# The last two groups of a fused decoder layer as expert chunks of their own, and the order of work after the last attention step

## What is computed

```python
x = _layernorm(x + attn(x))            # causal conv, minGRU scan, gelu feed-forward
x = _layernorm(x + xattn(x, ctx))      # cross attention, 16 heads of 64, causal mask
router = sigmoid(x @ gate_w + gate_b)  # 16 experts
values, indices = top_k(router, k=2)
values = values / sum(values)
x = _layernorm(x + shared_mlp(x) + sum_k values[k] * expert_mlp[indices[k]](x))
```

## Time and profile before

| | us |
|---|---|
| median of 3 runs | 1592.21 (1584.35 to 1595.37) |
| the profiled execution | 1589.19 |
| its span in the trace | 1587.5 |
| transposes of group 15 for the router begin (PE L417) | 1461.98 |
| slots of the last chunk written (DVE L1367) | 1476.67 |
| last scatter issued (POOL L1623) | 1496.18 |
| last `d_down` (PE L711) begins | 1537.13 |
| last gather issued (POOL L1635) | 1576.27 |

### The profile page before, as it was taken

The page is one execution under the profiler, slowest core; times in us unless marked ns, Lnnn a source line. Parts: engine busy times, 40 slices in busy tenths (PEclk is TensorE's granted clock), DMA queues, the critical chain, the costliest instruction groups (busy, mean ns, idle before and its releaser), DMA issues. The chain is left out here.

```text
span 1587.5 us, 34224 instructions
## 1 busy us (share of the span) xinstructions
PE 1327.4 (84%) x11168; PEld 1077.3 (68%) x11168; DVE 1021.0 (64%) x2723; ACT 876.1 (55%) x3255; POOL 834.0 (53%) x996
## 2 busy tenths in 40 slices
PE   2879797989899998989888998989889898986550
PEld 1667676777777776777777776867767777765540
DVE  3566657566756777667766767666776767666233
ACT  3656555565665665565655656565655655553120
POOL 4353334553446546664566545664566545564345
PEclk9999899999999999999999999999999999999685
DMA  6000000032112212132122212133122222133651
GB/s 211 8 7 8 7 8 14 10 92 81 36 57 69 84 57 60 47 105 85 36 63 83 81 54 65 44 94 95 36 65 76 81 64 64 33 95 104 183 156 46
DMA packets 142897, 105.78 MB, mean 67 GB/s; under 512 B 12352, under 2 KB 137856, under 8 KB 142720
## 3 DMA queue, kind: packets, MB, share of 16 engines
q1 hardware_dynamic: 132224, 84.71, 18.3%
q0 software_dynamic: 8192, 16.79, 3.6%
q10 hardware_dynamic: 2304, 2.10, 0.4%
HBM read 69.99 MB, written 33.55 MB: 65 GB/s over the span
## 5 line engine op out<-in xcount | busy, mean ns | idle before, releaser
L1595 POOL TENSOR_TENSOR pr<-pr,ri 128x480 f32<-128x480 f32 x256 | 250.4, 992 | 267.3 <-DVE ri L1229 265.3
L919 ACT ACTIVATE pr<-sE,nm 128x120 f32<-128x120 f32 x512 | 177.6, 359 | 292.1 <-DVE nm L1215 292.1
L591 PE MATMUL pvb<-pT,vv 120*64 120x128 f32 x2048 | 143.2, 283 | 42.9 <-DVE pT L1225 42.6
L919 ACT ACTIVATE pr<-sO,nm 128x120 f32<-128x120 f32 x512 | 178.8, 381 | 0.0
L558 PEld LDWEIGHTS sE<-kT,qT 64*128 64x128 f32 x1024 | 127.7, 193 | 54.8 <-issue 54.8
L591 PEld LDWEIGHTS pvb<-pT,vv 120*64 120x64 f32 x2048 | 112.5, 139 | 72.5 <-DVE pT L1225 55.3
L1635 POOL DMA_INDIRECT gat<-sorted_y,slot x128 | 127.1, 993 | 64.3 <-issue 47.1
L1623 POOL DMA_INDIRECT sorted_x<-x,slot x128 | 128.1, 1001 | 49.4 <-issue 34.6
L558 PE MATMUL sE<-kT,qT 64*128 64x120 f32 x1024 | 151.6, 290 | 0.0
L558 PE MATMUL sO<-kT,qT 64*128 64x120 f32 x1024 | 151.6, 290 | 0.0
L417 PE MATMUL t<-ident_f,pr 128*120 128x128 f32 x1024 | 146.6, 290 | 1.8 <-POOL pr L1595 1.4
(11 more groups left out here) (334 smaller groups left out, 3535.5 us busy)
## 6 DMA issues: line engine op xcount, KB each, us to landing
wq<-in_w_e SPq DMA_DIRECT2D x224, 128.0 KB
sorted_y<-yq SPq DMA_DIRECT2D x64, 256.0 KB, 2.5
xq<-sorted_x SPq DMA_DIRECT2D x56, 256.0 KB, 2.8
xt<-in_x SPq DMA_DIRECT2D x16, 256.0 KB, 3.0
sorted_x<-yq SPq DMA_DIRECT2D x16, 256.0 KB, 4.0
out_y<-y SPq DMA_DIRECT2D x64, 64.0 KB, 1.6
cT<-in_ctxT SPq DMA_DIRECT2D x16, 240.0 KB, 3.0
sorted_x<-x,slot POOLq DMA_INDIRECT x128
```

The source lines that it names most:

```text
L591: ins = mm(pvb[r * DK:(r + 1) * DK, (k // 2) * T:(k // 2 + 1) * T], vv[:, q, h * DK:(h + 1) * DK], pT[:, 4 * r + k // 2, :], start=True, s ...
L919: ins = f(pr[:, p % RING, r, i, :], score_banks[r][:, i * S:(i + 1) * S], ACT.Exp, bias=nm[:, p % 2, r, i:i + 1], accum_out=rsum[:, p % 2, ...
L1595: GP.tensor_tensor(pr[:, p % RING, r, :, :], pr[:, p % RING, r, :, :], ri[:, p % 2, r, :, :].to_broadcast([P, 4, S]), ALU.mult).then_inc(s ...
```

## The change

**Chunks.** Groups 0 to 13 keep their seven chunks of two groups. Groups 14 and 15 become a chunk each (`LONE`), of 24 tiles, six quads: quads 56 to 61 are group 14, quads 62 to 67 group 15. So the last two groups have 12 quads where they had 8. Slots, ranks and scatters of such a chunk are over four sequences (8 scatters).

**Step 15.** It now does all eight quads of chunk 6 (48 to 55), one per sub-step from 2 to 9 (`up_in`), with `d_down` into a bank of its own (`ma`), so that `d_up` no longer waits for `d_y` of the quad before. `c_slots` of group 14 is done at sub-step 1, and its eight scatters at sub-steps 3 to 6. On SP the loads of weights stand ahead of the stores of the sums. At its sub-steps 8 to 10 SP loads the rows of quads 56 to 59 and the weights of 56 to 58.

**After the attention.** There is no step 16. Every engine has a list written out: stage C of group 15 with quads 56 to 59 between its pieces, then the other quads and the sums of groups 12 to 15 (`TAIL` = 12). The sums there have buffers of their own (`gat_last`, `ys_last`, `y_last`), four sequences at a time, and `e_ln4` makes the reciprocal roots of four at once. The sorted outputs are in three memory buffers instead of two. ACT loads the weights of quads 65 to 67.

```diff
+LONE_TILES = 24
+DEEP = G // 2 - 2
+LONE = G // 2 - 1
+LAST = LONE * TILES // QUAD
+LONE_QUADS = LONE_TILES // QUAD
+END = LAST + 2 * LONE_QUADS
+TAIL = G - 4
...
+        def x_last_in(n):
+            i = n - LAST
+            return ("xq_last0", LONE_QUADS) if i < LONE_QUADS else (f"xq_last{1 + (i - LONE_QUADS) // 3}", 3)
+        def w_last_in(n):
+            i = n - LAST
+            return ("wq_last0", 3) if i < 3 else ("wq_last1", 3) if i < LONE_QUADS else (f"wq_last{2 + (i - LONE_QUADS) // 3}", 3)
...
+        def up_in(d, s):
+            if d is None:
+                return None
+            if d == G - 4:
+                return QUADS * d + s - 2 if 2 <= s < 2 + 2 * QUADS else None
+            return QUADS * d + s // 2 - 1 if s % 2 == 0 and 2 <= s <= 2 * QUADS else None
...
+                if d == G - 4:
+                    n = QUADS * d
+                    for s in range(2, PAIRS + LAG + 1):
+                        if n + s < LAST:
+                            x_load(n + s)
+                        if s > 2:
+                            if n + s - 1 < LAST:
+                                w_load(n + s - 1)
+                            d_store(n + s - 3)
+                        for e, q in sums_in(es, s - 1):
+                            e_store(e, q)
+                        if s == 8:
+                            for name in ("a_bank", "ln1_out"):
+                                sp.wait_ge(sem[name], whole(name, G - 1))
+                            for i in range(4):
+                                x_load(LAST + i)
+                        if s >= 8:
+                            w_load(LAST + s - 8)
...
             pipeline(body)
+            n = LAST + LONE_QUADS
             for i in range(2):
+                sp.wait_ge(sem["dT"], upto("dT", 0, LAST - 2 + i))
+                x_load(LAST + 4 + i)
+            w_load(LAST + 3)
...
             def d_T(n, c=None):
                 if last(n):
-                    pe.wait_ge(sem[f"xq_last{(n - LAST) // 4}"], 64)
+                    pe.wait_ge(sem[x_last_in(n)[0]], 16 * x_last_in(n)[1])
...
             def d_up(n, c=None):
                 if last(n):
-                    pe.wait_ge(sem[f"wq_last{(n - LAST) // 2}"], 32 * QUAD)
+                    pe.wait_ge(sem[w_last_in(n)[0]], 16 * QUAD * w_last_in(n)[1])
...
             pipeline(body)
-            for i in range(quads + 2):
+            c = G - 1
+            d_down(LAST - 1)
+            d_T(LAST)
+            d_T(LAST + 1)
+            c_x2_T(c)
+            d_up(LAST)
+            c_router_shared(c)
+            d_up(LAST + 1)
+            d_down(LAST)
+            c_shared_T(c)
+            d_T(LAST + 2)
+            d_up(LAST + 2)
+            d_T(LAST + 3)
+            c_rank(LONE + 1)
+            c_shared_down(c)
+            d_down(LAST + 1)
+            d_up(LAST + 3)
...
             pipeline(body)
-            for e in (G - 4, G - 2):
-                for j in range(0, 2 * SEQ + 2, 2):
...
+            gathers([TAIL], 0, 2 * SEQ)
+            for n in range(2 * SEQ):
+                c_scatter(LONE + 1, n)
+            e_ln4(TAIL)
+            gathers([TAIL + 1], 0, 2 * SEQ)
+            gathers([TAIL + 2], 0, SEQ)
+            e_ln4(TAIL + 1)
+            gathers([TAIL + 2], SEQ, 2 * SEQ)
+            gathers([TAIL + 3], 0, SEQ)
+            e_ln4(TAIL + 2)
+            gathers([TAIL + 3], SEQ, 2 * SEQ)
+            e_ln4(TAIL + 3)
```

More of the change, by code:

```diff
@@ L192, in layer_kernel @@
         wide = 2 * I + P
[L193 to L196, removed]
-        hq_last = gin[:, 0:2 * P].rearrange("p (v n) -> p v n", v=2)
+        half = QUAD * P
@@ L741, in body @@
                         b_scores(b, s)
-                    if D and s > 1 and odd:
-                        d_down(QUADS * d + (s - 3) // 2)
-                    if D and s > 1 and not odd:
-                        d_up(QUADS * d + s // 2 - 1, c)
+                    if up_in(d, s - 1) is not None:
+                        d_down(up_in(d, s - 1))
+                    if up_in(d, s) is not None:
+                        d_up(up_in(d, s), c if s == 2 else None)
                     if A and s == 8:
@@ L759, in body @@
                         c_shared_down(c)
-                    if C and s == 1 and c % 2:
-                        c_rank(c // 2)
-                    if D and odd and s < 9:
-                        d_T(QUADS * d + (s - 1) // 2, c)
+                    if C and s == 1 and closes(c):
+                        c_rank(chunk_of(c))
+                    if up_in(d, s + 1) is not None:
+                        d_T(up_in(d, s + 1), c if s == 1 else None)
                     if A and s == 8:
@@ L782, in _ @@
             pipeline(body)
-            for i in range(quads + 2):
-                if i < quads:
-                    d_T(LAST + i)
-                if 0 < i <= quads:
-                    d_up(LAST + i - 1)
-                if i > 1:
-                    d_down(LAST + i - 2)
+            c = G - 1
[15 more added lines that the diff above has]
+            d_up(LAST + 3)
+            for n in range(LAST + 4, END + 2):
+                if n == LAST + LONE_QUADS:
+                    d_down(n - 2)
+                    d_down(n - 1)
+                if n < END:
+                    d_T(n)
+                if n > LAST + LONE_QUADS:
+                    if n <= END:
+                        d_up(n - 1)
+                    if n > LAST + LONE_QUADS + 1:
+                        d_down(n - 2)
+                elif n < LAST + LONE_QUADS:
+                    d_down(n - 2)
+                    d_up(n)
         @block.scalar
@@ L1366, in c_slots @@
                         dve.wait_ge(sem[f"gath{q}"], whole(f"gath{q}", 2 * (k - 3) + 1))
[L1367 removed]
+                V.tensor_copy(slot[k % 3][:, :, some], sf[:, :, some]).then_inc(sem["slots"], 1)
             def d_act(n):
@@ L1456, in body @@
                         c_base(c)
-                    if C and s == 1 and c % 2:
-                        c_slots(c // 2)
-                    if D and s > 1 and not odd:
-                        d_act(QUADS * d + s // 2 - 1)
+                    if C and s == 1 and closes(c):
+                        c_slots(chunk_of(c))
+                    if up_in(d, s) is not None:
+                        d_act(up_in(d, s))
                     for e, q in sums_in(es, s - 1):
```

440 lines of the change are left out of this document (275 added, 165 removed).

## The result

The changed kernel takes 1584.47 us (median of 6 runs, 1581.79 to 1587.23), the kernel before on the same chip 1592.5 (1584.35 to 1595.37): a ratio of 0.9956, 95% interval 0.9935 to 0.9977. Run again beside some of the experiments, it stood at 0.9959 (0.9944 to 0.9975). So it is 0.4% faster, 5.6 us by the later medians and 8.0 by the first, which is "within 1%", the likeliest of the three; the forecast was 1580. The profiled execution has a span of 1581.6 us, where the sum said 1575.5 and before it was 1587.5.

The account below looks back on a forecast made before the run. The end was taken as bound by a chain of hand-overs, no engine full. Points timed in sequence gave a span of 1575.5 against 1587.5 (−12), 1577.2 profiled, 1580 on the median's scale; range 1564 to 1594.

Parts of the forecast that it names:

- (a): Step 15, sub-step 1: group 14's slots are new there, partly hidden by DVE idle time; +2.3 us, bounds 0.7 to 3.3.
- (b): Step 15: `d_act` at every sub-step instead of every second, 0.79 us at sub-steps 3, 5 and 7; +2.4 us.
- (c): Step 15: additional PE work, some 3 us per sub-step pair, hidden while PE waits for exponentials; uncovered up to 3 per pair.
- rival 3: Step 15: the loop of weights sets the pace, each of six sub-steps 2.8 us more; +17, 1597 us; chance 0.08.
- (d): Step 15, sub-steps 3 to 6: eight scatters on POOL, 2.5 us per sub-step, hidden by slack; 0, at most 1 us.
- `d_down(53)` and the list of SP: `d_down(53)` ends at 1453.7; SP then issues loads and stores to 1476.6, rows land 1480.0, PE stalls about 13 us.
- Rows to slots: From landed rows at 1480.0 to group 15's slots at 1501.1: 1.8 + 19.3 us, at a granted clock of 0.50.
- rival 2: Step 15 hardly grows and PE runs at full clock soon after the stall; −4 and −5, 1571 us; chance 0.17.
- Quads 57 to 59: After group 15's ranks: `d_y(57)` out at 1502.9, `d_y(59)` at 1517.1, with copies 7.1 us apart.
- Rows of 62 to 64: After the stores and weights in SP's list: third load of rows starts at 1523.0 and lands at 1526.4.
- Last six quads and last gathers: Kernel's end: last quads take 26.7 us, stored at 1553.1; last gather starts at 1563.3, span ends at 1575.5.
- Rival 1: After step 15: transfers, not SP's issuing, set the loads' pace; everything from 1480.0 up to 13 us earlier, 1567; chance 0.12.

## Why the prediction was right, and which of its steps were off

The median came out 4.5 us above the forecast, inside the range, and the likeliest class was the right one. By its steps, all on the old clock:

- **(a), slots in step 15:** predicted +2.3, measured +2.64.
- **(b), `d_act` at every sub-step:** predicted 0.79 each; 0.72 in the run with the scatters moved away.
- **(c), more PE work:** 0, as predicted. In step 15 PE waited 8.4 us for DVE's copies and never for a load (1395 to 1470); rival 3, weights as the pace, did not come.
- **(d), scatters at 0: the step that failed.** They cost 6.2 us by sub-step 7, 2.0 to 2.1 in each of the three intervals that hold a stretched instruction. "Whose next instructions have a sub-step of slack" was wrong: a cycle of POOL is roots, two gathers, two scatters, two multiplications and the root's wait for DVE's statistics (`mv`), and with the scatters it takes 8.9 and 11.0 us where the pace had been 7.5. The stretched `y` of the earlier trace rows was in my hands as a sign of that coupling, and I took it for a cost of `y` instead of a cost that grows when POOL is late.
- **`d_down(53)` and the list of SP.** It ended at 1459.6 (1457.68 + 1.94) instead of 1453.7. SP began the weights of 55 only 2.35 us behind it, where 0.7 had been taken, since a store of a sum stood ahead of them whose `y` was the 2.43 us one. From the end of their issue (1463.67) to the load of the rows of 61 (begun at 1486.2) the list took 22.6 us where 18.6 were summed: 1.2 more for the two stores, 1.5 more for the rows of 56 to 59, and 1.1 in gaps of 1.4 and 1.1 ahead of the weights of 57 and 58 where 0.7 had been taken. The landing took 3.5, where 3.4 had been taken. So `d_T(56)` began at 1491.7, not 1480.0. The mechanism (a list that delays the router through one semaphore) was right; of the 11.6 us by which the point was missed, 5.9 came from step 15 and 5.7 from the list. PE reached the point later too, so the stall itself was only 3 us longer than forecast.
- **Rows to slots:** 16.9 us (1489.71 to 1506.6) instead of 21.1. The lower clock lasted only to 1495; this is the second half of rival 2 (full clock soon after the stall), and it gave 4 back.
- **Quads 57 to 59:** on the old clock `d_y(57)` was out at 1508.2 instead of 1502.9 and `d_y(59)` at 1524.9 instead of 1517.1, the copies 9.6 and 7.2 us apart where 7.1 had been taken twice; PE waited 2.46 us for the weights of 59 to 61, which share a semaphore.
- **Rows of 62 to 64:** the third load began 7.9 us late, and then landing took 6.7 us instead of the 3.4 of the median in the earlier trace rows, in the stretch with a DMA share of 1.00. `d_T(62)` at 1537.7 instead of 1526.4.
- **Last six quads and last gathers:** 24.7 us to the first gather of group 15 (1560.40) where 26.7 were summed, then 10.2 to the last gather (10.25 predicted), and 11.0 to the end of the span, where 12.2 had been taken.
- **The sum:** span 1581.6 against 1575.5, or 8 us more on the old clock. `d_T(62)` was 11.3 us late; the shorter end paid 3.2 of it back.

That the median came so near is in part luck: step 15 and SP's list were 11.6 us too short in the sum, and the clock, for which the sum had taken the slow level throughout, and the end were too long in it. The chances also hold a slip: rivals 1 and 2 had 0.12 and 0.17, which is 0.29, not 0.27, and with a quarter of 0.63 it makes 0.45 for "faster", not 0.42. The order of the classes stays.

Rival 1 (loads don't hold up the router) is settled: the stall was 16.15 us, and taking its semaphores apart, once step 15 was repaired, gave 8 to 10 us. Nor were the transfers the pace of that list: from 1463.7 to 1486.7 the DMA share was 0.61 at 171 GB/s, where it reaches 1.00 at 264 later. On the rule that speaks for it: the Trainium skill ("DMA: Bandwidth & Descriptors", Issuing engines are not separate DMA queues) has the sequencer's time "usually small relative to the DMA itself". Here a quad's weights took 3.64 us to issue, and the rows of 61 landed 3.5 us after their issue began; and giving one quad's weights to ACT went with 4.9 us less on another chip, with runs that overlap. The trace doesn't agree with it for a list of twelve such DMAs. That page also says that all queues end on the same 16 DMA engines, and with it the share of 1.00 from 1528 to 1540 agrees.

On DVE beside POOL: POOL's pair of multiplications stretched `y` and `ys` to 2.42 to 2.55 us, and did not stretch the instructions with an input in PSUM that lay beside them (copies and maxima 0.65 to 0.69, `d_act` 0.42). The Trainium skill ("SBUF — State Buffer", Who interferes with whom) says that a DVE instruction with two inputs in SBUF contends with a GpSimd instruction that reads SBUF, and that the one that comes second waits for the whole of the other. By that rule, the trace agrees in that `ys` is held to their end. It doesn't show who came first: by the recorded starts `ys` did, by 0.42 and 0.46 us, and it was held for both multiplications. `y` reads only one tile and was held all the same, 2.42 us, of which that sentence says nothing. The prediction had asked only whether the scatters themselves stretch DVE's work. `ys` they don't stretch, and `x` by 0.2 to 0.3 us in two places; what I missed is that they move the multiplications.

## What to carry to other kernels

Work added to an engine with "slack" moves what stands behind it; ask beside what that will then run, and put the addition directly behind the instruction that the loop waits for, not ahead of it: the same eight scatters cost 6.2 us of step 15 in one place of the queue and 0.8 in the other, and the totals are 8 us apart. One semaphore for a batch of loads makes the first consumer wait for the last of them; give the load that something critical stands behind a count of its own. And a gain at the end of a kernel is judged by the whole list that now feeds it: here 36 us were saved behind the last slots and 32 paid ahead of them.

## What the runs showed of the hardware

- A DVE instruction of 0.35 us became one of 2.5 us at two POOL multiplications of 0.97 us each in a row, and ended with the second. I had allowed 0.7 us for it.
- Indirect DMAs being issued on POOL (1.0 us each) did not slow `ys` beside them (0.34 and 0.35 us); the scaling `x` took 0.54 and 0.60 us beside a scatter where it takes 0.34 elsewhere.
- After a pause of 16 us PE's granted clock was 0.50 for the next 5 us and 1.00 from 1495 to 1500; before, it was 0.50 throughout 1466 to 1470 after a pause of 2.67 us.
- On two other chips the kernel before took 1645 and 1642 us instead of 1589, and in the traces from there two quads' weights took 5.1 to 9.0 us each to issue between 1535 and 1561, where at most 4.7 was seen in step 15 and behind it on the first two.
